# First edge phase of a two-layer graph network: score sums and messages of two tile pairs in one VectorE instruction each, four message buffers instead of two

## What is computed

```
x = x + L0_gnn(layernorm(x))   # attention over edges, 8 heads of 32, graph norm, gelu
x = x + L0_ffn(layernorm(x))   # 8 experts, top 2
x = x + L1_gnn(layernorm(x))   # graph attention, 4 heads of 64
x = x + L1_ffn(layernorm(x))   # 8 experts, top 1 with a capacity
```

```
score = einsum('ehd,ehd->eh', q[dst], k[src]) / sqrt(32)
alpha = exp(score - segment_max[dst]) / segment_sum(exp)[dst]
out   = segment_sum(alpha[..., None] * v[src], dst)
```

## Time and profile before

| what | value |
|---|---|
| median of three executions | 8015.15 us |
| the three | 8013.78, 8015.15, 8033.4 us |
| span of the profiled execution, first to last instruction | 8018.8 us |
| busy over that span | PE 81%, PEld 61%, DVE 68%, ACT 55%, POOL 56% |
| first edge phase (343.8 to 3008.6 us of the span) | 2664.8 us |
| in it: PE 2439.1, DVE 2518.2, ACT 2007.3, POOL 1888.5 us busy | |

### The profile page before, as it was taken

The page is one execution under the profiler, slowest core; times in us unless marked ns, Lnnn a source line. Parts: engine busy times, 40 slices in busy tenths (PEclk is TensorE's granted clock), DMA queues, the critical chain, the costliest instruction groups (busy, mean ns, idle before and its releaser), DMA issues. The chain is left out here.

```text
span 8018.8 us, 128424 instructions
## 1 busy us (share of the span) xinstructions
PE 6511.0 (81%) x33506; PEld 4918.1 (61%) x33506; DVE 5451.2 (68%) x14605; ACT 4403.9 (55%) x12878; POOL 4452.1 (56%) x4481
## 2 busy tenths in 40 slices
PE   8899999999999987238966887888878787589995
PEld 5566666666666665237854555555555555577874
DVE  6599999999999997762256666666666666723333
ACT  2477777777777763214524666666666664222221
POOL 3277777777777750374413777777777774511110
PEclk9999999999999998559977888888898887599997
DMA  7777777777777762654465444444444444355556
GB/s 205 184 191 194 193 192 194 193 193 193 193 193 190 193 160 89 203 167 143 137 222 179 108 108 108 108 108 107 108 109 107 108 108 93 103 171 174 176 172 211
DMA packets 806962, 1260.55 MB, mean 157 GB/s; under 512 B 284271, under 2 KB 565287, under 8 KB 806055
## 3 DMA queue, kind: packets, MB, share of 16 engines
q0 software_dynamic: 273888, 837.38, 37.7%
q1 hardware_dynamic: 519637, 402.16, 17.5%
q10 hardware_dynamic: 12738, 12.80, 0.5%
HBM read 1057.07 MB, written 198.23 MB: 157 GB/s over the span
## 5 line engine op out<-in xcount | busy, mean ns | idle before, releaser
L667 POOL DMA_INDIRECT att_kv<-kv,att_idx x1872 | 1892.4, 1011 | 883.0 <-issue 660.8
L667 POOL DMA_INDIRECT gat_att_vst<-ft,gat_att_idx x1872 | 1822.6, 974 | 835.6 <-issue 535.3
L745 PE MATMUL gat_att_pag<-gat_att_msg,gat_att_S 128*128 128x260 f32 x3744 | 1242.8, 462 | 195.4 <-DVE gat_att_msg L950 188.1
L745 PE MATMUL att_pag<-att_msg,att_S 128*128 128x264 f32 x3744 | 1086.5, 413 | 57.0 <-DVE att_msg L950 38.6
L745 PEld LDWEIGHTS gat_att_pag<-gat_att_msg,gat_att_S 128*128 128x128 f32 x3744 | 759.1, 225 | 457.2 <-DVE gat_att_msg L950 330.1
L703 PE MATMUL att_pqd<-sum_acc,att_ST 128*128 x3744 | 981.8, 385 | 18.7 <-DVE att_prod L934 5.2
L745 PEld LDWEIGHTS att_pag<-att_msg,att_S 128*128 128x128 f32 x3744 | 637.0, 190 | 352.8 <-DVE att_msg L950 290.2
L703 PEld LDWEIGHTS att_pqd<-sum_acc,att_ST 128*128 128x128 f32 x3744 | 705.6, 191 | 134.9 <-issue 32.2
L789 ACT CAST gat_att_ST<-gat_att_pST 128x256 bf16<-128x256 f32 x936 | 348.4, 372 | 752.2 <-PE gat_att_pST L680 693.2
L950 DVE TENSOR_TENSOR att_msg<-att_vst,att_alpha 128x528 f32<-128x528 f32 x936 | 656.1, 701 | 17.3 <-DVE att_fl L875 0.7
L934 DVE TENSOR_TENSOR att_prod<-att_kv,att_pqd 128x512 f32<-128x512 f32 x936 | 632.8, 676 | 44.3 <-DMA att_kv<-kv,att_idx 34.1
(11 more groups left out here) (482 smaller groups left out, 12007.8 us busy)
## 6 DMA issues: line engine op xcount, KB each, us to landing
sexp_w<-in_L_ffn_w_dram SPq DMA_DIRECT2D x112, 1024.0 KB
att_kv<-kv,att_idx POOLq DMA_INDIRECT x1872
gat_att_vst<-ft,gat_att_idx POOLq DMA_INDIRECT x1872
top_row<-tok SPq DMA_DIRECT2D x106, 258.0 KB, 3.0
kv<-front_row SPq DMA_DIRECT2D x49, 520.0 KB, 3.5
gat_yg<-ytok SPq DMA_DIRECT2D x14, 1792.0 KB
sexp_row<-stok SPq DMA_DIRECT2D x56, 260.0 KB, 4.8
ft<-gat_row SPq DMA_DIRECT2D x14, 910.0 KB
```

The lines of the kernel that those rows point to most:

```text
L667: pool.indirect_dma_start(row, None, rows_t, IndirectOffsetOnAxis(ap=idx[:, k, 2 * p + i:2 * p + i + 1], axis=0)).then_inc(s_g[p % R], 16)
L745: t = pe.matmul(pag[p % 2][:, 0:AW], S[:, gs % RG, 2 * p + i, :], msg[:, p % 2, i, :], start=(i == 0), stop=(i == 1))
```

## The change

In the first edge phase (`U = 2`, `MB = 4`; the second has `U = 1`, `MB = 2`, as before) `reduce` runs at odd p alone and sums the products of both pairs, 128x1024 elements, in one instruction; `message` runs at even p alone and makes the messages of two pairs, 128x1056 elements, in one instruction, into two of four buffers. The counts of the semaphores for scores and messages go by double pairs. `products` waits at even p for the `reduce` of the two pairs ahead of it, which now stands right before it in VectorE's order; before, it waited for the `reduce` of two pairs back.

```
--- before.py
+++ after.py
@@ -522,6 +522,7 @@
     CD, NCP = 3, 4
+    U, MB = (1, 2) if gat else (2, 4)
...
-        msg = m.sb("msg", [P, 2, 2, AW])
+        msg = m.sb("msg", [P, MB, 2, AW])
...
-                        pe.wait_ge(s_score, h * GP + GP)
+                        pe.wait_ge(s_score, (h * GP + GP) // U)
...
                 def aggregate(g, gs, p):
                     T = g * GP + p
-                    pe.wait_ge(s_msg, T + 1)
+                    pe.wait_ge(s_msg, T // U + 1)
...
-                        t = pe.matmul(pag[p % 2][:, 0:AW], S[:, gs % RG, 2 * p + i, :], msg[:, p % 2, i, :],
+                        t = pe.matmul(pag[p % 2][:, 0:AW], S[:, gs % RG, 2 * p + i, :], msg[:, p % MB, i, :],
...
-                    wait(act, s_msg, g * GP + p - VR * GP + 1)
+                    wait(act, s_msg, (g * GP + p - VR * GP) // U + 1)
...
                     else:
-                        wait(v, s_score, T - 1)
+                        if p % U == 0:
+                            wait(v, s_score, T // U)
...
                 def reduce(g, gs, p):
                     v.wait_ge(s_front, g * GP + p + 1)
-                    v.tensor_reduce(score[:, gs % 2, :, 2 * p:2 * p + 2].rearrange("p h i -> p i h"),
-                                    prod[:, p % 2, :].rearrange("p (i h o) -> p i h o", i=2, h=H),
+                    t = slice(2 * (p + 1 - U), 2 * p + 2)
+                    v.tensor_reduce(score[:, gs % 2, :, t].rearrange("p h i -> p i h"),
+                                    prod[:, :, :].rearrange("p a (i h o) -> p (a i) h o", i=2, h=H),
                                     AX.X, ALU.add).then_inc(s_score, 1)
 
                 def message(g, gs, p):
 
-                    T = g * GP + p
+                    T, t = g * GP + p, slice(2 * p, 2 * p + 2 * U)
                     if p == 0:
                         v.wait_ge(s_alpha if gat else s_ca, g + 1)
-                    wait(v, s_agg, T - 1)
-                    v.tensor_tensor(msg[:, p % 2, :, 0:H * VH].rearrange("p i (h o) -> p i h o", h=H),
-                                    vst[:, gs % VR, 2 * p:2 * p + 2, 0:H * VH].rearrange("p i (h o) -> p i h o", h=H),
-                                    alpha[:, gs % 2, :, 2 * p:2 * p + 2].rearrange("p h i -> p i h").unsqueeze(
-                                        3).to_broadcast([P, 2, H, VH]), ALU.mult).then_inc(s_msg, 1)
+                    wait(v, s_agg, T + U - MB)
+                    v.tensor_tensor(msg[:, p % MB:p % MB + U, :, 0:H * VH].rearrange("p a i (h o) -> p (a i) h o", h=H),
+                                    vst[:, gs % VR, t, 0:H * VH].rearrange("p i (h o) -> p i h o", h=H),
+                                    alpha[:, gs % 2, :, t].rearrange("p h i -> p i h").unsqueeze(
+                                        3).to_broadcast([P, 2 * U, H, VH]), ALU.mult).then_inc(s_msg, 1)
...
                         work(1)
-                        if sends:
+                        if sends and up % U == 0:
                             message(ug, us, up)
                         work(3)
                         work(4)
                         if adds:
                             add(vg, vs, vp, p == 0)
                         work(5)
-                        if front and not gat:
+                        if front and not gat and p % U == U - 1:
                             reduce(g, gs, p)
```

## The result

The changed kernel takes 8226.68 us (median of 4 runs, 8217.38 to 8243.72), the kernel before 8016.05 beside it: ratio 1.0259, 95% interval 1.0244 to 1.0273. The forecast was 8200, range 8020 to 8290, slower with 0.78. The profiled execution took 8217.38 us, its span is 8215.7; before it was 8018.8.

What follows compares the result with a forecast made beforehand. VectorE was taken to lead, with PE about 0.2 us to spare per step. Terms of 0.87, 0, 0.48 and 0.05 us gave 1.40 per group, 164 us over 117, plus 20 for clock: 8015 + 184, about 8200 us, range 8020 to 8290.

Steps and rivals of the forecast that it cites:

- What merging saves: First edge phase: merged reduce takes 1.13 us and message 1.16, so each double pair saves 0.13 us, 61 us in all.
- Wait 1, reduce to product: At p = 0, 2 and 6 the product waits for the reduce right ahead of it, 0.12 us each.
- Wait 2, message to add through PE: The add waits for PE behind the message: +0.48 us at p = 4/5, +0.05 us at p = 6/7.
- X late: At p = 0/1 chain 0 on VectorE waits about 0.85 us for X from ScalarE, instead of 0.32.
- The bare load: At p = 1 the add's register load lies uncovered behind chain 0, costing 0.60 us.
- Clock: First edge phase: PE idles longer, so one group in three has a clock dip, 39 x 0.52 = 20 us.
- Balance: Rival, chance 0.12: PE and DVE settle in another phase, PE's path covered, load hidden; 7996 us, up to 8035.
- Faster: Rival, chance 0.10: an instruction's fixed part is larger than the distances say; 7879 us, half-way case 7954.
- One stall alone: Rival, chance 0.08: only p = 4/5 and 6/7 pay, less 0.13 at p = 0/1; 47 us, 8062.
- What the prediction said of gathers: Gathers are unchanged; each waits for the product four pairs back, which comes later, not earlier; no cost given.

Runs made afterwards that it cites:

- e10: The kernel before, with only the product's wait changed to the reduce right ahead of it, written last of its three waits: ratio 1.0136, 8121.93 us.
- e12: The kernel before, with the product waiting for the reduce right ahead of it, written first of its three waits: ratio 1.0060, 8063.36 us.
- e8: The change's merged reduce alone, with messages one per pair in two buffers: ratio 1.0152 against the kernel before, 8133.34 us.
- e9: The change's merged message alone in four buffers, with one reduce per step and the old wait: ratio 1.0073 against the kernel before, 8060.08 us.
- e7: The changed kernel with the register load for the odd step's add issued one step earlier: ratio 1.0190 against the kernel before, 8163.15 us.
- e3: The changed kernel reordered, merged message behind the reduce at odd p and register load behind that message: ratio 1.0085 against the kernel before, 8086.07 us.

## Why the prediction was right

**The direction and the size.** +184 us were forecast, 211 measured. The mechanism held at each place named; two sizes were too small, the wait of the product for the reduce and the clock.

- *What merging saves.* Forecast 1.13 and 1.16 us from start to start. The merged reduce takes 1.11 where L913 stands behind it (1374.75 to 1375.86), the merged message 1.17 (1376.69 to the add at 1377.86). The fixed part is small, as the distances said: two reduces at 0.60 became one of 1.11, a saving of 0.09, and two messages at 0.62, their usual distance, one of 1.17, a saving of 0.07. The Trainium skill ("VectorE: DVE Perf Modes", the side-by-side table of cycles) gives about 158 cycles at 0.96 GHz on top of the elements for one instruction, which would be 0.70 us for 512 elements and 1.23 for 1024, an estimate. The trace agrees for the length of one within 0.03 us, 0.68 and 1.20 to 1.22; as the price of an instruction among others that follow each other it is about twice what was saved here.
- *Wait 1, reduce to product, was mis-sized.* The step "0.08 + 0.04 = 0.12 us" took the 0.04 from an add with two waits, of which the one met last, for the rescale, is written first; the product has three, and the one met last was written last. It costs 0.21 to 0.24. From reduce to product it is 1.35 us in each of the three places, where 1.13 + 0.12 = 1.25 were forecast. Three times 0.1 us is the whole difference between the forecast group of 23.74 us and the measured 24.05, some 35 us in 117 groups. e10 and e12 show it by itself: 0.21 or 0.12 for the same wait, by its place in the list.
- *Wait 2, message to add through PE.* Forecast at 3.27 after the even product with a double step of 4.92; the add stands at 1379.37 - 1376.08 = 3.29. PE waits show 77.7 us where "some 60" were forecast. That p = 7 is covered by the rescale held too (3.23, no wait). e8 and e9 add that either half alone leaves it covered in most groups, though not in all: e8's own rows above come from a group in which the add at p = 5 had waited 0.32 us.
- *X late.* Chain 0 was forecast 3.62 after the group's first product; it stands at 1365.68 - 1362.06 = 3.62. The `turn` was forecast at 0.82 and came at 0.76. X's wait, forecast 0.85, is 0.76 there. It is not met in every group: 76 times, 52.1 us in all, against 104 times and 40.5 us before. In 39 of the 41 groups without it the product of p = 1 had already waited for its gather. So the mean group pays 0.85 us at p = 0/1 (6.59 for 5.74, in the table below), not the 0.98 of the quiet one; that this is so near the forecast of 0.87 is partly luck, as the wait for the reduce was too small in it.
- *The bare load.* Forecast 1.20 from chain 0 to the add, measured 1366.89 - 1365.68 = 1.21. e7 shows that the load is the cause of 0.38 of the 0.60 us that the prediction gave it; the rest did not go with it.
- *Clock.* PE was forecast to stand about 1.6 us before the message of p = 2; the row at 1370.56 has 1.40. The granted clock fell from 0.99 to 0.97. The prediction took one group in three with a dip, 39, at 0.52 us each, 20 us. The trace of the change has 38 of 114 groups with a mean granted clock under 1.00 (0.93 or 0.87; the group of the earlier trace rows, with its one dip to 0.50, has 0.93), the kernel before 3. So the count was right. But these groups are 0.90 us longer than the others, 25.01 against 24.11, and most of it, 0.67, lies at p = 4/5, where the add waits for PE and a slower PE is felt at once. 35 such groups more than before at 0.90 make some 32 us, an estimate, as a group with a dip may be long for another reason too.

**The rivals.** Balance asked for under 0.92 us from message to add; the message ends at 1376.69 + 1.25 = 1377.94, the add starts at 1379.37: 1.43. *Faster* asked for a larger fixed part: 1.11 for 1024 elements excludes it. *One stall alone* falls with the 0.98 us at p = 0/1. What the prediction said of gathers, that later products leave them no worse, was too simple: the uneven steps raised the product's wait for them in this phase from 34.1 us to 56.4. In e8 it is 77.7, 44 us more than before in a kernel that takes 126 us longer; in e3 it is 119.6, and that rise of 86 us is more than e3's whole loss of 75.

**The two halves.** e8 and e9 add up to 126 + 53 = 179 us, the change to 207 on that scale (0.0259 x 8007). Where the two differ shows in all groups of the phase (distances between the starts of the products, without the first two groups and the last; means over the groups with a granted clock of 1.00, to leave out the dips):

| double step, us | before | change | e8, reduce alone | e9, message alone |
|---|---|---|---|---|
| p = 0/1 | 5.74 | 6.59 | 6.21 | 5.82 |
| p = 2/3 | 7.43 | 7.46 | 7.53 | 7.36 |
| p = 4/5 | 4.45 | 5.05 | 4.59 | 4.36 |
| p = 6/7 | 4.90 | 5.01 | 5.06 | 5.19 |
| group | 22.51 | 24.11 | 23.39 | 22.73 |
| groups with that clock, of 114 | 111 | 76 | 70 | 81 |

At p = 4/5 the change pays 0.60 us and the two halves together 0.05: that is the stall that only both make. At p = 6/7 it is the other way round, 0.11 against 0.45, because in the message alone the first product of a group waits for its gather, 0.29 us in the mean. In all, the halves cost 0.88 + 0.22 = 1.10 us a group and the change 1.60; 0.50 in 117 groups would be 58 us. Over whole kernels the gap is only 28 us. The halves ran on another chip than the change, and the change's untouched rest was 17 us shorter; what else makes up the 30 us was not tried apart.

## What to carry to other kernels

Before merging two instructions, measure what they cost from start to start, not by their lengths: here 0.08 us a pair was to be had, and the consumer of the merged message got its first input 0.55 us later. Then ask of each merged instruction what it used to hide: a register load, a wait for another engine, an instruction between a producer and its consumer on the same engine. When an instruction has several waits, try the one that will be met last as the first written; here that was tried on one instruction alone.

## What the runs showed that was not expected

The place of a wait among an instruction's three is worth 0.09 us each time: 0.81 or 0.72 us from reduce to product, 1.0136 or 1.0060 for the kernel. The kernel before takes 8007 to 8016 us on some chips and 9370 on another, and an added wait that costs 1.4% elsewhere did not slow it there (0.9967). A change of this kind has to be compared on the same chip, and what it is worth on one need not hold on another.
